# A four-layer kernel's second stage: no loop, the tile scores spread between VectorE's other instructions, semaphores where drains stood

## The reference, cut to what matters

```python
x = x + mamba(layernorm(x))                                  # first stage of the kernel
x = x + einsum("btd,rde->bte", layernorm(x), factors) / sqrt(8) + bias
x = x + rms_norm(lightning_attention(rotary(q), rotary(k), v)) @ Wo   # q, k, v from layernorm(x)
# last layer, called on n = layernorm(x3), where x3 is x by now
xf = layernorm(n) * gamma + beta
tile_scores = sign(xf) @ tile_sigs.T      # best cluster of 8 tiles, then best tile in it
x_slice = xf[chosen tile's 8 channels]    # its min and max are taken over all tokens of a tile
x = x3 + n + (spline of x_slice, in those 8 channels of the token)
```

## Time and profile before

| what | value |
|---|---|
| median of 3 runs | 5924.46 us (5921.22 to 5928.32) |
| the profiled execution, its own time | 5923.98 us |
| its span | 5922.2 us |
| first stage and weights, up to the first norm of the second stage | to 3898.5 us |
| second stage | 3898.5 to 5666.0 us |
| `finish` | 5666.0 to 5922.2 us |
| busy in the second stage: PE, DVE, ACT, POOL | 1470.0, 1447.7, 417.5, 639.5 of 1767.5 us |

### The profile page before, as it was taken

One profiled execution on the slowest core, in us unless ns is written; L12 is line 12 of the kernel. 1 busy time (PEld: TensorE's weight loads), 2 busy tenths in 40 slices (PEclk: granted clock), 3 DMA queues, 4 the chain that ended last, 5 costly groups with the idle time before them and its releaser, 6 DMA issues. The chain is left out here.

```text
span 5922.2 us, 110904 instructions
## 1 busy us (share of the span) xinstructions
PE 5088.3 (86%) x41157; PEld 3047.7 (51%) x41157; DVE 4925.7 (83%) x7468; ACT 2610.0 (44%) x4180; POOL 3231.1 (55%) x1675
## 2 busy tenths in 40 slices
PE   6899999999999999999999998668888888888822
PEld 3444444444444444444444444246666777777722
DVE  3888988888888889889888888568888888888888
ACT  3655655655556556556556555212222222222200
POOL 1676676676766766766766767423333333333323
PEclk9999999999999999999999999879999998899855
DMA  2221222222222222212222222220000000000034
GB/s 84 76 101 65 100 99 74 94 87 79 101 81 85 101 79 86 95 72 101 90 76 101 85 81 94 91 86 25 20 22 22 20 23 20 24 20 20 18 111 138
DMA packets 139954, 421.27 MB, mean 71 GB/s; under 512 B 38368, under 2 KB 39904, under 8 KB 106592
## 3 DMA queue, kind: packets, MB, share of 16 engines
q1 hardware_dynamic: 136672, 411.75, 19.8%
q10 hardware_dynamic: 2816, 3.51, 0.2%
HBM read 361.99 MB, written 53.22 MB: 70 GB/s over the span
## 5 line engine op out<-in xcount | busy, mean ns | idle before, releaser
L335 POOL TENSOR_TENSOR s<-s,Cb 128x1024 f32<-128x1024 f32 x1024 | 2393.7, 2359 | 1083.8 <-DVE state L656 1073.0
L651 DVE TENSOR_TENSOR_SCAN s<-s,state,BU 128x512 f32<-128x512 f32 x2048 | 2452.7, 1260 | 425.4 <-PE BU L737 391.5
L501 ACT ACTIVATE s<-dt,ch 128x512 f32<-128x512 f32 x2048 | 1305.6, 712 | 778.6 <-PE Y L754 777.1
L754 PE MATMUL Y<-s,ident 64*64 64x512 f32 x8192 | 1011.8, 609 | 76.2 <-POOL s L335 75.3
L683 PE MATMUL PJ<-xnT,w_in 128*128 128x512 f32 x2048 | 946.9, 606 | 9.1 <-ACT dtuT L367 5.7
L737 PEld LDWEIGHTS BU<-spread,dtuT 32*128 32x128 f32 x16384 | 512.7, 189 | 528.4 <-DVE s L651 403.0
L737 PE MATMUL BU<-spread,dtuT 32*128 32x128 f32 x16384 | 611.2, 286 | 145.5 <-DVE s L651 140.8
L683 PEld LDWEIGHTS PJ<-xnT,w_in 128*128 128x128 f32 x2048 | 370.1, 190 | 479.0 <-issue 424.2
L754 PEld LDWEIGHTS Y<-s,ident 64*64 64x64 f32 x8192 | 279.3, 134 | 571.5 <-issue 533.8
L728 PE MATMUL PJ<-w_out,u 128*128 128x512 f32 x1024 | 472.8, 606 | 8.2 <-ACT xnT L371 6.7
L1110 POOL TENSOR_TENSOR x1t<-x1t,bias_b 128x512 f32<-128x512 f32 x64 | 81.1, 1267 | 525.8 <-DVE xa L1282 525.8
(11 more groups left out here) (218 smaller groups left out, 7634.8 us busy)
## 6 DMA issues: line engine op xcount, KB each, us to landing
Cb<-bc SPq DMA_DIRECT2D x256, 1024.0 KB, 4.9
res<-in_x SPq DMA_DIRECT2D x64, 256.0 KB, 4.9
x<-res SPq DMA_DIRECT2D x64, 256.0 KB, 5.2
x1t<-x SPq DMA_DIRECT2D x64, 256.0 KB, 2.6
out<-r_t SPq DMA_DIRECT2D x64, 256.0 KB, 2.0
xt<-in_x SPq DMA_DIRECT2D x31, 512.0 KB, 5.5
x_all<-out SPq DMA_DIRECT2D x16, 512.0 KB, 4.2
scm<-out SPq DMA_DIRECT2D x16, 512.0 KB, 4.6
```

The source lines that it names most:

```text
L335: nc.gpsimd.tensor_tensor(pair, pair, Cb[q % 2][:, 2 * part * T:2 * part * T + 2 * T], ALU.mult).then_inc(z_ready, 1)
L501: nc.scalar.activation(s[k % SLOTS][:, n, :], dt[p % 2][:, gi, :], ACT.Exp, scale=ch[:, 2 * p + gi, 7 + 4 * nq + n:8 + 4 * nq + n]).then_i ...
L651: nc.vector.tensor_tensor_scan(s[k % SLOTS][:, n, :], s[k % SLOTS][:, n, :], BU[:, n::4], state[:, b, k, n:n + 1], ALU.mult, ALU.add).then ...
L754: last_ = nc.tensor.matmul(Y[r][y_rows(r, gi), :], ident[rows, rows], s[(k_even + gi) % SLOTS][rows, n, :], start=False, stop=(n == 3 and ...
```

## The change

1. `steps` has no loop any more: all 70 steps are written out, on every engine.
2. On VectorE all 26 drains of a step's body are gone. Each producer increments a semaphore and each reader waits for it: `score_step` counts 17 increments a tile in the scores, others serve the norms (`stats_done`, `rd_ready`), x2 (`taken["ffn"]`), the rotary products, rrms and x3.
3. The 18 score instructions and the statistics of norms a, b and c no longer stand together. They are dealt out one or two at a time between the step's large instructions.
4. x3n is not made. Norm "d" is worked out from norm "c": its variance is var*rd*rd, its mean is 0, so one tiny instruction replaces the second statistics, and xf comes straight from x3 with the scale rd_c*rd_d (`rd_cd`).
5. r_t moves from GpSimd (an add of x3 and x3n) to ScalarE (one activation of x3 with scale 1+rd and bias -mean*rd, from two more tiny VectorE instructions), and stands there ahead of the copies of q, k and v; so do the roots for norms b and d.
6. The rotary products move behind `scm`, and `taken["wo"]` and `x3_ready` are given behind `kvu`.

```diff
-            for t in range(8):
-                body((None, t))
-            with eng.Fori(2, TILES // 4) as i:
-                for u_ in range(4):
-                    body((i, u_))
-            for t in range(TILES, TILES + LAST_STAGE):
+            for t in range(TILES + LAST_STAGE):
...
-                a = back(t, 5)
-                if valid(a):
-                    s_ = a[1] % 2
-
-                    wait(pool, S["x3n_ready"], num(a) + 1)
-                    if a[0] is not None or a[1] >= 2:
-                        pool.wait_ge(r_stored[s_], 16 * stored_count(a))
-                    nc.gpsimd.tensor_tensor(r_t[s_][:], x3[s_][:], x3n[s_][:], ALU.add).then_inc(S["r_ready"], 1)
...
-                    root("d", back(t, 5), 5)
+                    root("c", back(t, 5), 5)
+                if valid(back(t, 1)):
+                    root("b", back(t, 1), 1)
+                if valid(back(t, 5)):
+                    a = back(t, 5)
+                    s_ = a[1] % 2
+                    root("d", a, 5)
+                    wait(act, S["scale_ready"], num(a) + 1)
+                    if a[0] is not None or a[1] >= 2:
+                        act.wait_ge(r_stored[s_], 16 * stored_count(a))
+                    nc.scalar.activation(r_t[s_][:], x3[s_][:], ACT.Identity, bias=r_scale[s_][:, 1:2],
+                                         scale=r_scale[s_][:, 0:1]).then_inc(S["r_ready"], 1)
...
             def stats(n, x_):
-                nc.vector.bn_stats(ln[n][0][:], x_)
-                dve.drain()
+                nc.vector.bn_stats(ln[n][0][:], x_).then_inc(stats_done[n], 1)
+
+            def aggregate(n, a):
+                dve.wait_ge(stats_done[n], num(a) + 1)
                 nc.vector.bn_aggr(ln[n][1][:], ln[n][0][:]).then_inc(var_ready[n], 1)
+            def invert(n, a):
+                dve.wait_ge(sd_ready[n], num(a) + 1)
+                nc.vector.reciprocal(ln[n][3][:], ln[n][2][:]).then_inc(rd_ready[n], 1)
+
             def norm(n, a, x_, dst, done):
-                dve.wait_ge(sd_ready[n], num(a) + 1)
-                nc.vector.reciprocal(ln[n][3][:], ln[n][2][:])
-                dve.drain()
+                dve.wait_ge(rd_ready[n], num(a) + 1)
                 nc.vector.tensor_scalar(dst, x_, ln[n][1][:, 0:1], ln[n][3][:], ALU.subtract, ALU.mult).then_inc(done, 1)
...
+            def scored_to(a, step):
+                dve.wait_ge(score_step, num(a) * SCORE_STEPS + step)
...
+            def score_tiles(a):
+                scored_to(a, 1)
+                nc.vector.tensor_reduce(ts[:], pr[:].rearrange("p (i j) -> p i j", j=DS), AX.X, ALU.add
+                                        ).then_inc(score_step, 1)
...
+            def keep_extremes(a):
+                scored_to(a, 17)
+                dve.sem_inc(S["ohx_ready"], 1)
                 nc.vector.tensor_tensor(acc[:], acc[:], cand[:], ALU.max).then_inc(S["scored"], 1)
...
                 if valid(s1):
                     low("xT", s1, xaT)
-                if valid(s5):
-                    stats("c", x3[s5[1] % 2][:])
+                if valid(s6):
+                    score_products(s6)
                 if valid(s2):
                     low("x2T", s2, xbT)
+                if valid(s6):
+                    score_tiles(s6)
+                if valid(t):
+                    dve.wait_ge(x1_loaded[t[1] % 2], 16 * (stored_count(t) + 1))
+                    stats("a", x1t[t[1] % 2][:])
+                if valid(s6):
+                    score_clusters(s6)
...
+                    best_cluster(s6)
+                if valid(s5):
+                    stats("c", x3[s5[1] % 2][:])
+                if valid(s6):
+                    mark_cluster(s6)
                 if valid(t):
-                    dve.wait_ge(x1_loaded[t[1] % 2], 16 * (stored_count(t) + 1))
-                    stats("a", x1t[t[1] % 2][:])
+                    invert("a", t)
+                if valid(s6):
+                    lift_cluster(s6)
                 if valid(s5):
-                    s_ = s5[1] % 2
-                    wait(dve, S["r_ready"], num(s5) - 1)
-                    norm("c", s5, x3[s_][:], x3n[s_][:], S["x3n_ready"])
-                    dve.drain()
-                    stats("d", x3n[s_][:])
-                if valid(back(t, 6)):
-                    score(back(t, 6))
+                    aggregate("c", s5)
...
+                    best_tile(s6)
...
-                    dve.drain().then_inc(taken["ffn"], 1)
-                    nc.vector.bn_stats(ln["b"][0][:], x2[s1[1] % 4][:]).then_inc(S["x2_ready"], 1)
-                    dve.drain()
-                    nc.vector.bn_aggr(ln["b"][1][:], ln["b"][0][:]).then_inc(var_ready["b"], 1)
-                if valid(s2):
-                    s_ = s2[1] % 2
-                    dve.wait_ge(taken["k"], num(s2) + 1)
-                    dve.wait_ge(rot_loaded[s_], 16 * (stored_count(s2) + 1))
-                    wait(dve, S["qk_ready"], num(s2))
-                    pairs = qk[s_][:].rearrange("p q (h z j) -> p (q h) z j", h=HEADS, z=2)[:, :, :, 0:ROT]
-                    cos = rot[s_][:, 0, :].rearrange("p (z j) -> p z j", z=2)
-                    sin = rot[s_][:, 1, :].rearrange("p (z j) -> p z j", z=2)
-                    nc.vector.tensor_tensor(rc[:], pairs, cos.unsqueeze(1).to_broadcast([P, 2 * HEADS, 2, ROT]), ALU.mult)
-                    for z in range(2):
-                        last_ = nc.vector.tensor_tensor(
-                            rs_[:, :, z, :], pairs[:, :, 1 - z, :],
-                            sin[:, z, :].unsqueeze(1).to_broadcast([P, 2 * HEADS, ROT]), ALU.mult)
-                    dve.drain().then_inc(S["rot_parts"], 1)
+                                                   x1t[s1[1] % 2][:], ALU.mult, ALU.add).then_inc(taken["ffn"], 1)
+                if valid(s6):
+                    mark_tile(s6)
...
+                    mean, var, rd = ln["c"][1][:, 0:1], ln["c"][1][:, 1:2], ln["c"][3][:]
+                    dve.wait_ge(rd_ready["c"], num(s5) + 1)
+                    nc.vector.tensor_scalar(ln["d"][1][:, 1:2], var, rd, rd, ALU.mult, ALU.mult
+                                            ).then_inc(var_ready["d"], 1)
+                    nc.vector.tensor_scalar_add(r_scale[s_][:, 0:1], rd, 1.0)
+                    nc.vector.tensor_scalar(r_scale[s_][:, 1:2], mean, rd, -1.0, ALU.mult, ALU.mult
+                                            ).then_inc(scale_made, 1)
+                if valid(s6):
+                    mask_dims(s6)
...
+                    nc.vector.tensor_tensor(rd_cd[:], ln["c"][3][:], ln["d"][3][:], ALU.mult).then_inc(rd_made, 1)
...
+                    nc.vector.tensor_scalar(xf[s5[1] % 2][:], x3[s5[1] % 2][:], ln["c"][1][:, 0:1], rd_cd[:],
+                                            ALU.subtract, ALU.mult).then_inc(S["xf_normed"], 1)
...
-                    nc.vector.reciprocal(rrms[s_][:], rsum[s_][:])
-                    dve.drain()
+                    nc.vector.reciprocal(rrms[s_][:], rsum[s_][:]).then_inc(rrms_made, 1)
+                if valid(s2):
+                    s_ = s2[1] % 2
+                    dve.wait_ge(taken["k"], num(s2) + 1)
+                    dve.wait_ge(rot_loaded[s_], 16 * (stored_count(s2) + 1))
+                    wait(dve, S["qk_ready"], num(s2))
...
-                                                   ALU.mult, ALU.add).then_inc(taken["wo"], 1)
-                    dve.drain().then_inc(S["x3_ready"], 1)
+                                                   ALU.mult, ALU.add).then_inc(x3_made, 1)
                 if valid(s3):
                     dve.wait_ge(filled["kvu"], num(s3) + 1)
                     wait(dve, S["kv_ready"], num(s3))
                     nc.vector.tensor_tensor(kvu[:].rearrange("p k n -> p (k n)"), bank("kvu")[:],
                                             kv_mask[:].rearrange("p k n -> p (k n)"), ALU.mult
                                             ).then_inc(taken["kvu"], 1)
-                    dve.wait_ge(taken["kvu"], num(s3) + 1)
-                    dve.sem_inc(S["kvu_ready"], 1)
+                if valid(s4):
+                    dve.wait_ge(x3_made, num(s4) + 1)
+                    dve.sem_inc(taken["wo"], 1)
+                    dve.sem_inc(S["x3_ready"], 1)
```

More of the change, by code:

```diff
@@ L1137, in body @@
                     wait(pool, S["kvd_ready"], num(a) + 1)
-                    wait(pool, S["kvu_ready"], num(a) + 1)
+                    wait(pool, taken["kvu"], num(a) + 1)
                     wait(pool, filled["at"], num(a) + 1)
@@ L1213, in body @@
                     take("v", a, vv[s_][:])
-                if valid(back(t, 1)):
-                    root("b", back(t, 1), 1)
                 if valid(back(t, 5)):
```

158 lines of the change are left out of this document (109 added, 49 removed).

## The result

| | before | after |
|---|---|---|
| median | 5924.22 us (4 runs, 5921.22 to 5928.32) | 5547.25 us (4 runs, 5545.57 to 5548.46) |
| ratio, 95% interval | | 0.9365 (0.9354 to 0.9376) |
| profiled execution, its span | 5923.98, 5922.2 us | 5545.57, 5543.6 us |
| filling, 58 full steps, emptying | 85.8, 1579.9, 97.6 us | 84.6, 1221.4, 78.1 us |
| one full step | 27.24 us | 21.06 us |

The windows of the profile after, in the columns of the earlier trace rows: filling, full steps, emptying, and what follows the stage.

The account below looks back on a forecast made before the run. VectorE was taken to set the 27.24 us step; its terms cut 26.99 to 20.1 us, and TensorE's floor made it 21.4. 5924 less 339 (58 full steps) and 12 (emptying) gave 5573 us, range 5545 to 5670.

Parts of the forecast that it names:

- TensorE then sets the step: Full steps: once VectorE's own step falls to 20.1 us, TensorE's 21.05 us is the floor.
- Item 1: VectorE's step start: its 1.60 us wait goes, since rc and rs behind `scm` lie under the chain there.
- Item 3: VectorE's drains: 24 counted at 0.16 us each return 3.8 us a step, bounds 0 and 4.8.
- The rule that was weighed: VectorE's drains: a pipeline flush follows every operation anyway, so removing drains returns nothing.
- Item 4: VectorE's xf, xb and rc: no longer beside GpSimd instructions, they return 2.6 us a step, bounds 1.0 to 2.6.
- Item 6: VectorE before x2: waiting for GpSimd's bias add adds 1.2 us of idle time a step.
- Item 7: VectorE's pr at the next step's start: collides with GpSimd's adds, 0 to 1.3 us, taken as 0.8.
- The waits in the queue: VectorE's queue: waits that take a second slot add an estimated 0.3 us a step, between 0 and 1.0.
- 0.8 us to spare: VectorE ends `scm` at 17.2 us, TensorE's last product would start at 18.0; step taken as 21.4 us.
- The emptying: Pipeline's last steps: the first three save 4, 4 and 3 us, the last ones 1; 12 us together.
- Rival 2: VectorE's waits cost what drains did: no drain gain, 23.9 us a step, 5724 us; 10%.
- rival 4: Slower: moved rotary products close a ring of 18.3 us; with 10 us more, 28.3 us a step, 5985 us; 3%.

Follow-up runs that it names:

- the lightened kernel: Changed kernel with only the high-by-high products of q, k and v, to take work off TensorE; 5388.04 us, ratio 0.9095.
- the block: Changed kernel without the low-part products of q, k and v, its 18 score instructions together again, with semaphores and no drains; 5493.66 us.
- two small edits: Changed kernel with the sum of squares in fp32r with two columns, and ScalarE's copy aTs moved behind xaT and xbT; 5487.28 us, ratio 0.9264.

## Why the prediction was right, and where its sizes were off

**Right: TensorE then sets the step, at 21.05 us.** The window of a filling step in the earlier trace rows gave the floor to 0.01 us: the full steps stand 21.06 us apart, with a busy TensorE for 98.8% (97 said), a clock of 1.00 and no wait for `scm`. The windows of the full steps alone would not have given it, since there TensorE's work took 22.9 us at a clock of 0.92.

**A limit that the prediction did not count: x2 and bank 5.** It read only the wait for `scm` from TensorE's queue. TensorE waited longer in total for x2, 2.2 us in every step. With x2 left 16.1 us into the step, the step could not fall under the ring of 24.2 us that the kernel with the moved rotary products shows, whatever VectorE saves behind x2. The change brings x2 forward from 16.1 to 7.2 us and so opens this ring. The forecast holds, but the sum of VectorE's terms alone does not say why the floor could be reached.

**Item 1, the start wait, came back,** as the item allowed: 2.58 us, since VectorE is the early one now. With the rotary products moved alone it fell from 117 us to 99.5 over the stage, not to 0. Its "issue" part, 38.2 us in the earlier trace rows, was the loop; without the loop these steps keep an ordinary start wait, so 23 us of it come back.

**Item 3, the drains, was a little too small.** 3.8 us taken, with an upper bound of 4.8. Added up over the full steps, the gaps between the instructions that both kernels have are 4.4 us a step shorter after the change. Putting 25 drains back costs 4.4 us of gaps (4.5 in the lightened kernel), and with what follows from them 5.1 in the lightened kernel. The rule that was weighed, the Trainium skill's "VectorE: DVE Perf Modes", section "The DRAIN you can't avoid", would have made it 0. (Its advice on operations and semaphores stands in the same page's "Rules for kernel authors".) Putting the drains back cost 177 us, so the measurement decides against carrying its eight copies over to this kernel. In part it holds: a semaphore link in one block is only some 0.04 us cheaper than a drained one. The larger part of a link's gain comes from what stands between, and a drain holds that back too.

**Item 4, the port, was right** to 0.1 us on all three instructions.

**Item 6, the new wait of x2, was wrong.** I took x2 to read what the bias add of the same step writes. It reads the tile of the step before, biased long ago; x2 starts 0.04 us before the add and VectorE idles nowhere there. What the add does is to hold `ohx`, the next instruction: 0.78 us where 0.25 is its length in the block and in the kernel before, so 0.5 and not 1.2. The Trainium skill's "SBUF — State Buffer", section "SBUF: two separate sides", has VectorE and GpSimd share one port pair that one of them holds for a whole instruction. The rows agree: `ohx` ends 0.05 us after the add. x2, with one input in PSUM, takes the usual 0.68 us beside the same add.

**Item 7, the collision of pr, was there**, 0.90 us where the instruction alone takes 0.39. But it was not new: pr took 0.70 in the earlier trace rows and 0.76 on the mean before, so the change added 0.14 us, and 0.8 was taken. The waits in the queue (0.3 taken) left no trace in VectorE's rows.

The terms close. The count gave VectorE's own step as 20.1 us, without a wait at its start; what it measured without its two waits is 17.65. Of the 2.5 us between, item 6 makes 0.7, item 7 0.7, the drains 0.6 and the waits in the queue 0.3. Another 0.3 is the sum of slightly shorter times of many instructions, which no item had.

**"0.8 us to spare", and so 21.4 us a step, failed.** This is the step of the working that cost most: 0.34 us a step, 20 of the 26 us. With VectorE 2.5 us quicker than counted, `scm` was no near thing in any step, and the clock did not leave 1.00. The emptying gave 19.5 us instead of 12: among its first three steps the starts of pr stand 17.8 and 18.3 us apart where they stood 22.9 and 23.1. So these two steps gave 10 us where 8 had been taken, and the other four gave 9.5 where 4 had been.

**Rivals.** Rival 2's time, 5724 us, is that of the changed kernel with its drains, 5724.04; its 23.9 us a step was measured too (23.93). That is partly luck, since its base was 2.5 us too high and its drains, with the collision of `acc` and the start wait, were too cheap. The ring of rival 4 did not bind, and the list of waits names no place in the full steps where TensorE idles but the 0.25 us ahead of the ones product.

Where the 377 us come from can't be split into items that add up. Alone on the kernel before, the loop gives 34 us and the rotary products' place 85. Taken out of the kernel after, the drains' removal gives 177 us, and the place or x3n nothing in the full steps. Each is cut off in turn, by TensorE's floor or by the ring through x2.

## What to carry to other kernels

Look for a stretch, such as the filling of a pipeline, where the second engine already does all its work and the bounding one does not: its length is the floor that the change can reach, better read than summed. When dependent small instructions follow one another on VectorE, put independent work between them and order them by semaphores; a drain holds back the independent work too, and can push it into a GpSimd instruction. Ask also which instruction in the queue another engine waits for, and bring that one forward; here it was x2. Once an engine's floor binds, edits elsewhere stop paying, and the next gain lies in that engine's own chain (here 60 us from two small edits).

## What the runs showed that I had not expected

- The 1221 us of full steps all ran at a granted clock of 1.00. It was 0.92 before, 0.96 with the drains back and 0.82 in the lightened kernel with drains. The lightened one's step is as long as that with the drains back (23.91 and 23.93 us), but its start wait is 0.4 us longer (1.13 against 0.74) and pr 0.4 shorter (0.72 against 1.13). So what the lower clock cost there can't be read from the equal steps:

```profile
3986.00:5350.00 1364.00, 1071.41 (x7988) 908.93 (x7987) 1145.00 (x2851) 402.61 (x915) 497.14 (x401) 0.82 0.08 25
```

- A 128x64 tensor_scalar of 0.18 us can last 1.32 us beside a GpSimd add: the length of the small instruction says nothing of what a collision costs.
- An fp32 product with a single column of ones is no small thing: its 8 records take 1.05 us, and 4 in fp32r with two columns take 0.60. From start to the next product's start it is 0.91 and 0.47 us.
